# An attention and expert kernel: the values' first piece and the transposition of the maxima change places, and the maxima are copied sooner

## The reference, cut to what matters

```python
Q, K, V = heads(x @ Wq), heads(x @ Wk), heads(x @ Wv)        # 16 heads of 8
scores  = einsum('bhqd,bhkd->bhqk', Q, K) / sqrt(8)
weights = softmax(where(causal, scores, -1e6), axis=-1)
x = layernorm(x + einsum('bhqk,bhkd->bhqd', weights, V) @ Wo + bo)
xn = layernorm(x) * gamma + beta
x = layernorm(x + sum over the top 2 experts e of gate_e(xn) * (gelu(xn @ W1[e] + b1[e]) @ W2[e] + b2[e]))
```

## Time and profile before

| | before |
|---|---|
| median of 3 runs | 985.86 us (982.15 to 987.94) |
| the profiled execution | 977.47 us |
| its span, first to last instruction | 975.7 us |
| busy: TensorE | 851.0 us (87%) |
| busy: VectorE | 734.4 us (75%) |
| busy: ScalarE | 681.5 us (70%) |
| busy: GpSimd | 662.7 us (68%) |
| granted TensorE clock, mean | 0.973 |

### The profile page before, as it was taken

One profiled execution on the slowest core, in us unless ns is written; L12 is line 12 of the kernel. 1 busy time (PEld: TensorE's weight loads), 2 busy tenths in 40 slices (PEclk: granted clock), 3 DMA queues, 4 the chain that ended last, 5 costly groups with the idle time before them and its releaser, 6 DMA issues.

```text
span 975.7 us, 28904 instructions
## 1 busy us (share of the span) xinstructions
PE 851.0 (87%) x9151; PEld 561.4 (58%) x9151; DVE 734.4 (75%) x2003; ACT 681.5 (70%) x1451; POOL 662.7 (68%) x911
## 2 busy tenths in 40 slices
PE   5688898988998999989989988779999999999950
PEld 2344354444444444444544544358999988989950
DVE  2887879888988888888899888964554565377756
ACT  2377687777787787777878877755666555668775
POOL 6243555778778778787787786658777656567654
PEclk9799999999999999999999999999999999999985
DMA  7625635636446455345345332253233223365644
GB/s 196 203 75 162 177 89 164 182 106 206 139 135 208 111 165 187 102 145 174 105 161 172 101 126 73 63 143 92 80 89 88 84 78 88 112 212 184 187 133 125
DMA packets 168787, 132.37 MB, mean 136 GB/s; under 512 B 52861, under 2 KB 154532, under 8 KB 168512
## 3 DMA queue, kind: packets, MB, share of 16 engines
q1 hardware_dynamic: 156352, 112.34, 38.8%
q0 software_dynamic: 8640, 17.06, 5.1%
q10 hardware_dynamic: 3648, 1.12, 0.5%
HBM read 71.42 MB, written 61.01 MB: 136 GB/s over the span
## 4 chain that ended last, share of the span: by engine, by line
PE 50%; POOL 17%; issue 11%; ACT 11%; DVE 6%; DMA 4%; SPq 0%; ACTq 0%; POOLq 0%; DVEq 0%
PE ring L1301 12%; PE ring L1285 12%; PE ps_v L1219 6%; PE ring L1156 4%; ACT probs L827 4%; POOL probs L683 4%; PE ring L1187 3%; POOL rows_d L725 3%; POOL rs L749 3%; DVE negmax L1345 2%; PE ps_m L1049 2%; PE ps_m L1055 2%; PE ps_m L1033 2%; PE ps_m L1044 2%; POOL qarea L647 1%
## 5 line engine op out<-in xcount | busy, mean ns | idle before, releaser
L1345 DVE TENSOR_REDUCE negmax<-ring 128x2 f32<-128x1024 f32 (+3 forms) x512 | 407.1, 813 | 62.5 <-PE ring L1202 61.3
L827 ACT ACTIVATE probs<-ring 128x768 f32<-128x768 f32 (+1 forms) x384 | 334.7, 879 | 109.2 <-PE ring L1156 104.9
L683 POOL TENSOR_SCALAR_AFFINE_SELECT probs<-probs 128x512 f32<-128x512 f32 x256 | 162.5, 638 | 149.4 <-ACT probs L827 147.4
L952 ACT ACTIVATE vpad<-ring,b_s 128x128 f32<-128x128 f32 x568 | 162.3, 368 | 105.4 <-PE ring L1285 102.4
L733 POOL DMA_INDIRECT y_d<-vpad,xs x142 | 148.1, 1043 | 81.5 <-DVE vpad L1660 52.0
L1219 PE MATMUL ps_v<-probs,vpad 128*32 128x512 f32 (+3 forms) x2048 | 182.0, 444 | 10.0 <-POOL probs L683 9.8
L1301 PE MATMUL ring<-qarea,vpad 128*128 x1136 | 153.8, 279 | 4.8 <-issue 2.7
L1285 PE MATMUL ring<-kside,w_t 128*128 128x128 f32 x1136 | 152.6, 277 | 1.1 <-issue 0.9
L725 POOL DMA_INDIRECT rows_d<-xn,slot x128 | 129.1, 1008 | 30.2 <-issue 26.3
L1301 PEld LDWEIGHTS ring<-qarea,vpad 128*128 128x128 f32 x1136 | 137.9, 192 | 10.0 <-issue 8.3
L1285 PEld LDWEIGHTS ring<-kside,w_t 128*128 128x128 f32 x1136 | 138.1, 192 | 3.9 <-issue 2.8
(11 more groups left out here) (201 smaller groups left out, 1178.4 us busy)
## 6 DMA issues: line engine op xcount, KB each, us to landing
kside<-qk_d SPq DMA_DIRECT2D x32, 512.0 KB, 4.8
qk_d<-qarea SPq DMA_DIRECT2D x32, 384.0 KB, 2.7
xs<-rows_d SPq DMA_DIRECT2D x142, 66.0 KB
qk_d<-qarea SPq DMA_DIRECT2D x32, 256.0 KB, 2.5
qarea<-qk_d SPq DMA_DIRECT2D x16, 512.0 KB
qodd<-qk_d SPq DMA_DIRECT2D x16, 512.0 KB
probs<-y_d SPq DMA_DIRECT2D x16, 512.0 KB, 5.1
xin<-L_attn_x SPq DMA_DIRECT2D x16, 256.0 KB, 3.5
```

What stands on the lines that cost most here:

```text
L683: pool.affine_select(out=diag, in_=diag, pattern=[[0, 4], [1, P]], compare_op=ALU.is_ge, fill=0.0, base=0, channel_multiplier=-1).then_inc ...
L827: nc.scalar.activation(of_unit(h // 2, part), ring[:, 2 * part % 3, :, (0, P, P)[part]:S], ACT.Exp, scale=SCALE).then_inc(sem("exp_done"), 1)
L952: ins = nc.scalar.activation(ht[:, n % 4, c, :], ps_a[:, n % 4, c * P:(c + 1) * P], ACT.Gelu_apprx_tanh, bias=b1_s[:, bass.ds(e, 1), c:c + ...
L1345: ins = nc.vector.tensor_reduce(negmax[:, n // 6 % 2, qb, s:s + 2], ring[:, (2 * n + 1) % 3, :, c0:c0 + nk], AX.X, ALU.max, negate=True)
```

## The change

On TensorE, `values` with kb = 0 moves from the end of the step h % 4 == 1 to the end of the step h % 4 == 0, behind maxima 1. mT moves within the step h % 4 == 1 from behind maxima 2 to ahead of scores 2. The values' wait for the masks becomes one for every call of `values`, and asks for one mask less unless the call holds kb = 2. On ScalarE, `copy_max` moves from u = 2 to u = 0 of its step, ahead of the first normalization and the exponentials of the odd step, and `place_max` from u = 1 of the next step to u = 2 of the same step. No instruction is added or dropped.

```diff
                         if h == 5 and u == 0 and nxt.exists(NB):
                             copy_v(act, nxt)
+                        if u == 0 and h % 4 == 1:
+                            copy_max(act, *((i, 1), (i, 2), (i, 3), (nxt, 0))[h // 4])
...
-                        if u == 2 and h % 4 == 1:
-                            copy_max(act, *((i, 1), (i, 2), (i, 3), (nxt, 0))[h // 4])
                         if u == 1:
                             middle(act, h, i, nxt, prev, rb)
-                            if h % 4 == 2:
-                                place_max(act, *((i, 1), (i, 2), (i, 3), (nxt, 0))[h // 4])
+                        if u == 2 and h % 4 == 1:
+                            place_max(act, *((i, 1), (i, 2), (i, 3), (nxt, 0))[h // 4])
...
+                need(pe, sem("masked"), NH, b, GH * (g + 1) - (kbs[-1] < 2))
                 if kbs[0] == 0:
-                    need(pe, sem("masked"), NH, b, GH * (g + 1))
...
+                    if h % 4 == 1:
+                        misc(i, *MISC[h])
                     scores(i, h // 2, 2 if h % 2 else 0)
                     maxima(mb, mu + (2 if h % 2 else 0), i, h)
-                    if h in MISC:
+                    if h in MISC and h % 4 != 1:
                         misc(i, *MISC[h])
...
-                    if h % 4:
+                    if h % 4 != 1:
                         vb, vg = (i, h // 4 - 1) if h >= 4 else (i.plus(-1), 3)
-                        values(vb, vg, ((0,), (1,), (3, 2))[h % 4 - 1])
+                        values(vb, vg, ((0,), None, (1,), (3, 2))[h % 4])
```

## The result

The changed kernel takes 1004.48 us, the median of 4 runs (1001.4 to 1004.93). The kernel before, run beside it on the same chip, takes 984.46 (982.15 to 987.94). The ratio is 1.0185, with a 95% interval of 1.0147 to 1.0223, so the change costs about 18 us. The prediction said 1011 (981 to 1024).

The account below looks back on a forecast made before the run. TensorE was taken as fullest, busy 34.75 of 37.94 us a block. Blocks 2 to 14 at 1.97 each (25.6), plus 2.9 for blocks 0, 1 and 15, less 3.5 for the transfer: +25.0, so 1011 us (981 to 1024).

Parts of the forecast that it names:

- Removed waits: TensorE's waits in a block's first three groups, for VectorE, the last mask and exponentials: 1.82 us a block if nothing replaces them.
- M1's 0.62 in A: Wait of the second maxima piece in a block's first group: 0.62 us, stays, as the values come only behind it.
- A: Group from head step 0 of a block: two stalls vanish but return as a wait of the next maxima; -0.04 us.
- B: Group from head step 4: transposition waits for V's copy, then maxima copy and normalization delay the exponentials; +0.61 us.
- C: Group from head step 8: transposition starts as before, the third score piece's exponentials end 0.81 us later; +0.60 us.
- D: Group from head step 12, without normalization there: VectorE gets the third maxima late, with layer-norm statistics behind; +0.80 us.
- The transfer of the maxima: Small DMA issued 0.4 to 2 us sooner, shortening TensorE's waits in score steps; -3.5 us, bounds 0 and 6.7.
- The ends: Blocks 0, 1 and 15, with few or no normalizations: half a block's price each, 2.9 us together.
- The total: Whole kernel: 25.6 + 2.9 - 3.5 = +25.0 us, giving 1011 us.
- The stalls go and nothing comes back: Rival: third score piece's exponentials end before the next maxima need them; -30 us, 956 us; chance 0.15.
- VectorE everywhere: Rival: VectorE passes its delay on in every group, not only the last; +43 us, 1029 us; chance 0.08.

Follow-up runs that it names:

- e5: The kernel before with only the values' smaller wait for the masks; 982.79 us, ratio 0.9983.
- e1: The changed kernel with ScalarE's order as before (late copy of the maxima and late transfer), TensorE's new order kept; 1003.46 us, ratio 1.0161.
- e2: The kernel before with only ScalarE's order changed (early copy of the maxima, its transfer right behind); 1011.78 us, ratio 1.0267.
- e3: The kernel before with only the values' first piece moved to the end of the group's first step and the smaller mask wait; 986.3 us, ratio 1.0027.
- e4: The changed kernel with the values' first piece back behind the maxima; early transposition, early copy and smaller mask wait kept; 996.52 us, ratio 1.0108.
- e6: The kernel before with early transposition and copy of the maxima in each block's first group only, plus the smaller mask wait; second chip, 1034.93 us, ratio 0.9883.
- e12: The kernel before with early transposition and copy in the first group only, smaller mask wait, and GpSimd's gamma product at head step 6; 966.64 us, ratio 0.9808.
- e11: The changed kernel with GpSimd's product with gamma at head step 6 instead of 5; second chip, 1060.64 us, ratio 1.0136.

## Why the prediction was right, and where its sizes were off

Direction and mechanism held. In front of the exponentials of S2 now stand V0, mT, the copy and, but for D, a normalization, and the next M0 pays.

- **Removed waits.** The mask wait went, and M1's 0.62 in A stayed, as said. e5 shows that the mask wait was cover: alone it is worth 0.09 of its 0.67.
- **A, predicted -0.04, measured -0.22.** The products of V0 held TensorE 0.88 us (396.24 to 397.12) where the prediction took 1.00, and the exponentials of S2 began 4.08 us into the group instead of 4.19.
- **B, predicted +0.61, measured +0.68.** mT waited 0.24 for the copy of V, and the exponentials of S2 began 4.88 into the group (predicted 4.85). The prediction blamed ScalarE's order. e1 and e2 show that either order alone costs B almost the same (+0.52 and +0.63), and together not the sum: S2's exponentials are late if S2 stands behind mT on TensorE, or if they stand behind the copy on ScalarE.
- **C, predicted +0.60, measured +1.07.** This is the mis-sized term, 0.46 of it. The replay said "mT waited for the copy of the attention and starts as before"; it started 3.38 us into the group and not 2.92. VectorE reached the group late, since its small gates product took 0.94 us, and the turn of the attention and mT's bank followed:

```profile
414.77 0.63 PE L1075 MATMUL ps_m<-ident,att 128*128 128x128 f32 x4 [0.22 <-DVE att L1387]
...
417.26 0.39 PE L1062 MATMUL ps_m<-identb,mhl 128*16 128x128 bf16 x4 [0.18 <-ACT attt L936]
...
419.40 0.39 PE L1187 MATMUL ring<-kside,qarea 64*128 64x512 bf16 x2 [0.94 <-ACT probs L827]
```

  The 0.6 of later work in B had pushed that product from 6.60 to 7.35 us after the group's start, into the stretch of GpSimd's gamma product; in blocks 2 and 3 C had 10.08, as predicted (block 2 has no gates product, and in block 3 GpSimd came to its own 6.35 us into the group, in block 9 6.99). The prediction had put nothing on this meeting of the two products.
- **D, predicted +0.80, measured +0.80.** The statistics do stand between VectorE's two parts, and the next S1 and S2 wait for it (0.18 and 0.16 us):

```profile
429.61 0.69 DVE L1347 TENSOR_REDUCE negmax<-ring 128x2 f32<-128x512 f32 x1 [0.74 <-PE ring L1202]
...
430.31 0.86 DVE L1392 BATCH_NORM_STATS2 stats<-ysum 128x6 f32<-128x128 f32 x4
431.09 0.41 DVE L1347 TENSOR_REDUCE negmax<-ring 128x2 f32<-128x256 f32 x1
```

  V0 early alone costs 0.60 (e3), TensorE's two moves together 0.81 (e1), ScalarE's places nothing (e2), and neither does mT first with V0 left behind (e4).
- **The transfer of the maxima**, predicted -3.5: its waits behind the first fell by 3.1 us, and A of blocks 1, 2, 4 and 7, where they had been, came down by 0.53, 1.53, 1.24 and 0.59. Less A's usual 0.22 in the last three, that is 3.2. Right. At the kernel's first scores, which the sum left out, TensorE waited 2.8 us for the maxima before and 3.7 for the keys (kside) after.
- **The ends.** Predicted 1.0 each for blocks 0, 1 and 15 and 1.97 for 14; measured 0.8, 0.65, 1.3 and 1.05. Within block 15 the price moved: C was 9.20 before and 7.04 after, and D, up to its last scores, 8.28 before and 12.25 after, with TensorE waiting 1.73 us for the transfer of the attention rows and 2.57 for the routing's logits (1.45 before). C was 9.05 to 9.20 in before, e5 and e6, 7.87 in e4, and 6.8 to 7.2 in all the others. In the three long ones the granted clock was 0.50 for 3.4 us of that group, in all others 1.00 throughout it. Before's A of block 14 also ran at 0.50 for 3.4 us and took 9.85, against 8.90 after, which is why block 14 seems to cost so little. What comes behind block 15, at which the prediction put nothing, was 3.3 us shorter after; from its last scores on the kernels on the first and third chip took between 331.2 and 334.8, before 335.8 and after 332.5, so this need not be the change's doing.
- **The total.** Steady blocks cost 2.3 us and not 1.97; some ends cost less than predicted, and some early blocks were long before and had less to lose (C of blocks 3 and 4 took 9.73 and 9.74). By medians 18 to 20 us against 25; in the profiled spans 27. Without the 3.0 of the later start the spans differ by 23.9, against a predicted 25.0. That is nearer than the terms were, and in part luck: C's price was 0.46 a block too small, and the 3.3 us behind block 15 and the slow clock in before's blocks 14 and 15, which no term names, go the other way.
- **The rivals.** "The stalls go and nothing comes back" fails on the maxima pieces' waits, which grew from 23.2 to 63.9 us, except in A: there e6 and e12 show it, once V0 stays behind M2. "VectorE everywhere" holds for D alone, and C in another way than it named.

## What to carry to other kernels

A wait that is named in a profile may be cover for another engine's later wait; follow what is queued behind the late engine before pricing it (taking away 9.8 us of mask waits alone was worth some 1.7, which its interval does not tell from nothing). When a copy is placed ahead of a critical exponential, ask per stage whether its input is already there: in the one group where it was, and ScalarE idle anyway, the move gained 0.54 us (e4, A), and in those where its bank was still full it cost about twice that (1.01 in B, 1.07 in C, of which some may be GpSimd's gamma product). Try such an order by group rather than by a rule that holds for all.

## What the runs showed of the hardware that was not expected

- A VectorE product of 128x4 whose two inputs lie in SBUF took from 0.15 to 0.95 us in blocks 3 to 14 of the kernels before and after, and where it was long it ended within 0.02 us of the GpSimd instruction beside it (412.39 and 412.37; 171.69 and 171.68). In block 9 of e11 the one-hot product (128x32), beside two short GpSimd operations, took 1.33 us, against 0.18 in the kernel after. The Trainium skill, page "SBUF — State Buffer", section "🔬 SBUF: two separate sides", says that the port pair shared by VectorE and GpSimd is an exclusive lock, held for a whole instruction, between a GpSimd operation that reads SBUF and a VectorE operation with two SBUF inputs; these rows agree (the gamma product reads SBUF). If that is what holds the product, the trace shows the wait as a longer instruction and not as idle time.
- The clock was granted at 0.50 in five blocks of e2; in block 7 this came behind three idle stretches of TensorE, the longest 0.93 us, and V0's products took 1.94 us instead of 1.06. Block 9 of e2, with the same stretches, and block 9 of the kernel after, with waits of 0.94 us in three of its groups, ran at 1.00.
- The first group began between 37.8 and 42.2 us over the kernels, which is as much as many edits are worth.
